# Attention queries and keys in f16 halves, three-product scores, and a new split of the copies of the turned probabilities

## The reference

```python
q = (x @ Wq).reshape(N, S, HEADS, HEAD_DIM).transpose(0, 2, 1, 3)
k = (x @ Wk).reshape(N, S, HEADS, HEAD_DIM).transpose(0, 2, 1, 3)
...
logits = jnp.einsum('nhid,nhjd->nhij', q, k) * scale
causal = 1000000000.0 * (jnp.tril(jnp.ones((S, S), dtype=logits.dtype)) - 1.0)
logits = logits + causal[None, None, :, :]
attn = jax.nn.softmax(logits, axis=-1)
out = jnp.einsum('nhij,nhjd->nhid', attn, v)
```

## Time and profile before

| | |
|---|---|
| median of the runs shown | 890.14 us |
| profiled execution | 890.64 us |
| its span in the profile | 889.4 us |
| TensorE busy in the span | 859.9 us (97%) |
| VectorE busy | 606.1 us (68%) |
| ScalarE busy | 557.2 us (63%) |
| GpSimd busy | 377.8 us (42%) |

### The profile page before, as it was taken

How to read it: one execution, slowest core, us unless ns; L and a number is a source line. 1 busy time by engine, 2 the same in 40 slices (tenths; PEclk the granted TensorE clock), 3 DMA queues, 4 the chain that set the end, 5 groups by cost and what they waited for, 6 DMA issues and landing times. The chain is left out here.

```text
span 889.4 us, 23089 instructions
## 1 busy us (share of the span) xinstructions
PE 859.9 (97%) x8094; PEld 680.0 (76%) x8094; DVE 606.1 (68%) x1669; ACT 557.2 (63%) x1251; POOL 377.8 (42%) x492
## 2 busy tenths in 40 slices
PE   5999999999999999999999999999999999999996
PEld 3888788888888888767676666676788888887864
DVE  3667588776667675756666667869677767766655
ACT  4988776777676776655756565564455555555555
POOL 1634354343433475324444332544534444444433
PEclk9999999999999999999999999999999999999999
DMA  9733424342424331410000000399423323333226
GB/s 317 207 126 113 142 97 152 119 160 96 143 94 138 103 119 49 62 42 2 1 1 1 2 1 1 105 393 356 158 52 50 49 44 50 49 50 50 43 27 195
DMA packets 61579, 88.04 MB, mean 99 GB/s; under 512 B 17279, under 2 KB 46527, under 8 KB 61343
## 3 DMA queue, kind: packets, MB, share of 16 engines
q1 hardware_dynamic: 53439, 75.52, 25.8%
q0 software_dynamic: 7488, 10.27, 7.3%
q10 hardware_dynamic: 544, 0.79, 0.3%
HBM read 56.00 MB, written 30.56 MB: 97 GB/s over the span
## 5 line engine op out<-in xcount | busy, mean ns | idle before, releaser
L648 POOL TENSOR_SCALAR prob<-prob,rden 128x128 f32<-128x128 f32 (+1 forms) x256 | 122.9, 498 | 183.1 <-DVE rden L949 183.0
L2219 PE MATMUL ps<-slots,e 128*128 128x128 f16 x1872 | 190.0, 219 | 2.2 <-DVE xs L2386 2.1
L2219 PEld LDWEIGHTS ps<-slots,e 128*128 x1872 | 152.6, 97 | 35.3 <-issue 4.4
L843 ACT ACTIVATE prob<-prob,nmx 128x128 f32<-128x128 f32 (+1 forms) x256 | 113.2, 444 | 29.8 <-DVE nmx L943 29.8
L2227 PE MATMUL ps<-e,xT 128*128 x312 | 117.3, 378 | 0.0
L2316 ACT ACTIVATE slots<-slots 128x512 f32<-128x512 f32 x78 | 49.1, 630 | 106.8 <-DVE slots L2370 106.8
L943 DVE CUSTOM_DVE_ANT_0 prob<-ps,mask 128x128 f32<-128x128 f32 (+1 forms) x256 | 73.7, 353 | 41.5 <-PE ps L730 41.5
L31 PE MATMUL ps<-xT,wqkv 128*128 128x256 f16 x768 | 97.2, 278 | 2.0 <-ACT slots L850 1.4
L31 PEld LDWEIGHTS ps<-xT,wqkv 128*128 128x128 f16 x768 | 73.4, 99 | 18.3 <-issue 6.9
L1731 POOL DMA_INDIRECT xg<-rows_x,dst x39 | 40.9, 1049 | 106.3 <-DVE mask L2359 103.0
L2228 PE MATMUL ps<-e,xT 128*128 x312 | 85.0, 273 | 0.0
(11 more groups left out here) (267 smaller groups left out, 1855.3 us busy)
## 6 DMA issues: line engine op xcount, KB each, us to landing
halves<-parted SPq DMA_DIRECT2D x36, 512.0 KB, 2.9
piece<-in_L_ffn_ew SPq DMA_DIRECT2D x32, 512.0 KB, 4.5
e<-halves SPq DMA_DIRECT2D x16, 1024.0 KB, 15.2
piece<-in_L_ffn_sh_w SPq DMA_DIRECT2D x4, 512.0 KB, 8.8
sw<-halves SPq DMA_DIRECT2D x4, 512.0 KB, 6.8
rows_x<-xs SPq DMA_DIRECT2D x4, 512.0 KB, 7.4
xs<-back_y SPq DMA_DIRECT2D x8, 256.0 KB, 4.4
out<-xs SPq DMA_DIRECT2D x8, 256.0 KB, 2.1
```

Of the source, the lines that this page charges most:

```text
L648: PO.tensor_scalar(prob[u][:, h, r], prob[u][:, h, r], rden[u][:, h, t:t + 1], 1.0, ALU.mult, ALU.mult).then_inc(normed, 1)
L843: SC.activation(at, at, ACT.Exp, bias=nmx[u][:, h, t:t + 1], scale=-1.0, accum_out=den[u][:, h, t:t + 1]).then_inc(exped, 1)
L2219: yield PE.matmul(ps[:, 2 * u + q, (k % 4) * P:(k % 4) * P + P], w[ch][h], xgT[u][j][:, ch, :], start=n == 0, stop=n == 3 * DC - 1)
```

## The change

Queries and keys leave the PSUM bank as two f16 parts. ScalarE writes the high part, and a new VectorE operation subtracts it from the bank and writes the low part, after which the semaphore `qk_lo` says that the item is there and the bank is free. The scores are the three f16 products of `HILO` in place of one float32 product. ScalarE copies three of four heads' turned probabilities and VectorE one. On ScalarE the even item's copy stands ahead of the second pair's exponentials in all stages, and the squares of the context are spread over stages 4 to 9. On VectorE the odd item's low part stands behind `add_projection`, and the scaling of the context moves from stages 9 to 12 to stages 11 to 13.

```diff
@@ -312,6 +312,9 @@
 
         FOLDED = [(wb, wbh, r, slice(0, G3), WS) for r in range(DC)] + [
             (pnT, pnh, r, slice(k * half, (k + 1) * half), 1.0) for k in range(2) for r in range(DC)]
+        ROOTED_AT = 10
+        SQUARED_AT = {4: (0,), 5: (1,), 6: (2,), 7: (3,), 8: (4, 5), 9: (6, 7)}
+        SCALED_AT = {11: (0, 1, 2), 12: (3, 4, 5), 13: (6, 7)}
         FOLDED_AT = {26: (0,), 27: (1,), 28: (2,), 29: (3, 4), 30: (5,)}
 
         def folded_high(q):
@@ -461,7 +464,8 @@
             wo = [sb(c, f"wo{i}", [P, PAIRS, D], F16) for i in range(2)]
             bo = sb(c, "bo", [P, D])
             zrow = sb(c, "zrow", [P, D + 2])
-            qk = [part(slots_flat, 4 * 3 * DC * GT + 8 * S * i, 2 * S).rearrange("p (k t) -> p k t", k=2) for i in range(2)]
+            qk = [[part(slots_flat, 4 * 3 * DC * GT + 8 * S * u + 4 * S * i, 2 * S, F16).rearrange("p (k t) -> p k t", k=2)
+                   for i in range(2)] for u in range(2)]
             v_sb = [sb(c, f"v{i}", [P, S // P, 2, P]) for i in range(2)]
             prob = [sb(c, f"prob{i}", [P, 4, 384]) for i in range(2)]
             pT = sb(c, "pT", [P, 4, 384])
@@ -667,7 +671,7 @@
                         normalise(j + 1, 1)
                     if batch_ending(j) is not None and j < LAST:
                         root(batch_ending(j))
-                    if j == 8:
+                    if j == ROOTED_AT:
                         context_root()
                     for q in FOLDED_AT.get(j, ()):
                         folded_high(q)
@@ -704,7 +708,7 @@
                 def project_qk(n):
                     b, cols = n // PAIRS, slice(n % PAIRS * P, n % PAIRS * P + P)
                     if n >= 1:
-                        PE.wait_ge(qk_out, n)
+                        PE.wait_ge(qk_lo, n)
                     if n % PAIRS == 0:
                         PE.wait_ge(x_hi, b + 1)
                         PE.wait_ge(x_lo, b + 1)
@@ -723,12 +727,13 @@
                     if m >= 2:
                         PE.wait_ge(pT_out, 2 * (m - 1))
                     for p in range(2):
-                        PE.wait_ge(qk_out, 2 * m + p + 1)
+                        PE.wait_ge(qk_lo, 2 * m + p + 1)
                         for t in range(2):
-                            for h in range(2):
-                                r = slice(HD * h, HD * h + HD)
-                                mm = PE.matmul(ps[:, 2 + 2 * p + h, query_tile(t)], qk[p][r, 0, t * P:t * P + P],
-                                               qk[p][r, 1, 0:(t + 1) * P], start=True, stop=True)
+                            for n, (i, j) in enumerate(HILO):
+                                for h in range(2):
+                                    r = slice(HD * h, HD * h + HD)
+                                    mm = PE.matmul(ps[:, 2 + 2 * p + h, query_tile(t)], qk[p][i][r, 0, t * P:t * P + P],
+                                                   qk[p][j][r, 1, 0:(t + 1) * P], start=n == 0, stop=n == len(HILO) - 1)
                         mm.then_inc(s_mm, 1)
 
                 def weigh_values(m):
...
@@ -847,14 +852,14 @@
                     SC.wait_ge(qk_mm, n + 1)
                     if n >= 2:
                         SC.wait_ge(s_mm, n - 1)
-                    SC.mul(qk[n % 2][:, :, :], ps[:, 0, :].rearrange("p (k t) -> p k t", k=2), 1 / WS).then_inc(qk_out, 1)
+                    SC.mul(qk[n % 2][0][:, :, :], ps[:, 0, :].rearrange("p (k t) -> p k t", k=2), 1 / WS).then_inc(qk_hi, 1)
 
                 def probs_turned(m):
 
                     SC.wait_ge(p_turned, 2 * m + 2)
                     if m >= 1:
                         SC.wait_ge(o_mm, m)
-                    SC.copy(pT[:, 2:4, :], ps[:, 4:6, 0:384]).then_inc(pT_out, 1)
+                    SC.copy(pT[:, 1:4, :], ps[:, 3:6, 0:384]).then_inc(pT_out, 1)
 
                 def values_out(m):
                     SC.wait_ge(v_mm, m + 1)
@@ -885,24 +890,23 @@
                         vw_high(1)
                     if 0 <= j - 1 < STAGES:
                         heads_high(j - 1)
-                    if j <= 0:
+                    if j + 2 < STAGES:
                         queries_keys(2 * (j + 2))
                     if 0 <= j + 1 < STAGES:
                         exponentials(j + 1, 1)
-                    if 0 < j < STAGES - 2:
-                        queries_keys(2 * (j + 2))
                     if 0 <= j < STAGES:
                         probs_turned(j)
                     for q in high_at.get(j, ()):
                         piece_high(q)
-                    if SHARES <= j < 2 * SHARES:
-                        context_squares(2 * (j - SHARES))
-                        context_squares(2 * (j - SHARES) + 1)
+                    for b in SQUARED_AT.get(j, ()):
+                        context_squares(b)
                     if share_at(j) is not None and share_at(j) >= KEYS:
                         prep_scalar(share_at(j), 6)
+                    if j < 0:
+                        queries_keys(2 * (j + 2) + 1)
                     for i in HIGH_AT.get(j, ()):
                         weight_high(i)
-                    if j + 2 < STAGES:
+                    if 0 <= j < STAGES - 2:
                         queries_keys(2 * (j + 2) + 1)
                     if j == LAST - 1:
                         high_part(0)
@@ -943,6 +947,11 @@
                             VE.tensor_tensor_reduce(prob[u][:, h, r], ps[:, 2 + h, r], mask[:, r], -SCALE, HIGHEST,
                                                     ALU.add, ALU.min, nmx[u][:, h, t:t + 1]).then_inc(masked, 1)
 
+                def queries_keys(n):
+                    VE.wait_ge(qk_hi, n + 1)
+                    VE.scalar_tensor_tensor(qk[n % 2][1][:, :, :], ps[:, 0, :].rearrange("p (k t) -> p k t", k=2), 1 / WS,
+                                            qk[n % 2][0][:, :, :], ALU.mult, ALU.subtract).then_inc(qk_lo, 1)
+
                 def reciprocals(m, p):
                     u, h = m % 2, slice(2 * p, 2 * p + 2)
                     VE.wait_ge(exped, 8 * m + 4 * (p + 1))
@@ -953,7 +962,7 @@
                     VE.wait_ge(p_turned, 2 * m + 1)
                     if m >= 1:
                         VE.wait_ge(o_mm, m)
-                    VE.tensor_copy(pT[:, 0:2, :], ps[:, 2:4, 0:384]).then_inc(pT_out, 1)
+                    VE.tensor_copy(pT[:, 0, :], ps[:, 2, 0:384]).then_inc(pT_out, 1)
 
                 def heads_low(m):
                     slot = 2 * (m % DOUBLES)
@@ -1006,6 +1015,8 @@
                         reciprocals(j + 1, 0)
                     if 0 <= j - 1 < STAGES:
                         heads_low(j - 1)
+                    if j + 2 < STAGES:
+                        queries_keys(2 * (j + 2))
                     if 0 <= j < STAGES:
                         probs_turned(j)
                     if 0 <= j + 1 < STAGES:
@@ -1017,23 +1028,26 @@
                         prep_vector(share)
                     for q in FOLDED_AT.get(j - 1, ()):
                         folded_low(q)
+                    if j < 0:
+                        queries_keys(2 * (j + 2) + 1)
                     for i in LOW_AT.get(j, ()):
                         weight_low(i)
                     for n in low_shares.get((j, 1), ()):
                         piece_low(n)
+                    if batch_ending(j) is not None and j < LAST:
+                        add_projection(batch_ending(j))
+                    if 0 <= j < STAGES - 2:
+                        queries_keys(2 * (j + 2) + 1)
                     for n in low_shares.get((j, 2), ()):
                         piece_low(n)
                     if j == 5:
                         context_biases()
-                    if j == 8:
+                    if j == ROOTED_AT:
                         context_mean()
-                    if 9 <= j < 9 + NB // 2:
-                        context_scale(2 * (j - 9))
-                        context_scale(2 * (j - 9) + 1)
+                    for b in SCALED_AT.get(j, ()):
+                        context_scale(b)
                     if batch_turned(j) is not None:
                         inputs_low(batch_turned(j))
-                    if batch_ending(j) is not None and j < LAST:
-                        add_projection(batch_ending(j))
                 low_part(0)
                 add_projection(NB - 1)
                 vw_low(2)
```

4 lines of the change are left out of this document (2 added, 2 removed).

## The result

The changed kernel takes 899.65 us (median of 4 runs, 898.52 to 901.63), the kernel before 888.59 us beside it (4 runs, 886.86 to 892.16). The ratio is 1.0126 with a 95% interval of 1.0104 to 1.0148: slower by 1.3%, 11.1 us. I had forecast 896 us, 6 us more than before: the right side, in the range, and 5 us short of the 11.1 measured.

What follows compares the result with a forecast made beforehand. TensorE was taken to bound the kernel: scores -9.6, waits of before -4.9, new waits +15.3 and start +3.5 gave +4.3 us; a late load (0.5) and the clock (1.3) made it +6, so 896 us, range 882 to 904.

Steps and rivals of the forecast that it cites:

- the odd item's chain: ScalarE and VectorE, two-piece stages: second pair can start at 10.76 us, TensorE wants it at 9.82 to 10.68.
- The list of waits: TensorE's new waits by stage: 7.2 us in stages 2 to 9, 5.7 in 10 to 17, 2.4 from 18; together 15.3.
- The scores' term: Scores on TensorE: three f16 products take 0.99 us instead of 1.30, 0.30 less a step, 9.6 us in 32 steps.
- Late loads and the clock: Left out of the chains: a late load worth 0.5 us and a fallen clock worth 1.3, raising the sum to +6.
- The scaling of the context: VectorE, stages 12 to 14: scalings of 0.395 us each ahead of the masks do not fit, beside whh of 1.3 us.
- The start: Ahead of the loop: stage 1 starts 2.8 us late and waits another 0.75; 3.5 us more, bounds 0 and 4.
- waits of before: Losses of the kernel before in stages 1 to 9, taken to go: 4.9 us less.
- The rival with smaller waits: Waits in the 20 waiting stages are 0.3 us smaller each, the sum cancels: 890 us; chance of same 0.27.
- the rival with the low part hidden: VectorE's low part is hidden, only plain two-piece stages wait, some 4 us with the start: 881 us; chance 0.19.
- the rival in which the f16 halves do not overlap: Scores on TensorE cost 0.7 us more per stage, 22 us: about 913 us; f16 without its gain has chance 0.06.

Runs made afterwards that it cites:

- Experiments 2: The changed kernel with a stage's second piece on ScalarE behind the odd item's copy; 887.69 us, ratio 0.9986 to the kernel before.
- experiment 4: The changed kernel with squares, root and scaling of the context in the stages of the kernel before; 902.72 us, ratio 1.0155.
- experiment 3: The changed kernel with the odd item's low part ahead of `add_projection` on VectorE; 903.58 us, ratio 1.0153.
- experiment 8: The kernel before, without f16 parts, with only the second piece of a stage moved behind the odd item's copy; 885.98 us, ratio 0.9959.
- experiment 10: The changed kernel with second piece behind the odd copy, and root, scaling, weights' parts and quarter shares in other places; 884.66 us, ratio 0.9953.
- 6: The changed kernel with ScalarE and VectorE each copying two heads of turned probabilities; 898.00 us, ratio 1.0102.
- 5: The changed kernel with ScalarE's even copy back behind the second exponentials in the stages from 1 on; 905.25 us, ratio 1.0182.
- 7: The changed kernel with context work, heads' copies and even copy as before, low part kept; 908.12 us, ratio 1.0212.
- 1: The kernel before with f16 high parts alone and three high-by-high score products, no low part, not to reference precision; 879.33 us, ratio 0.9891.

## Why the prediction was right in kind and too small

**The mechanism held.** I had the odd item's chain (three heads' copy, two pieces, high part, low part) as what TensorE would wait for. It is the line that the waits name. In stage 15 the odd copy starts 9.43 us after the scores (predicted 9.38) and the low part ends at 10.73 (10.76). I had stages 18 to 25 nearly free of waits, and only stage 25 has one, of 0.34. The list of waits, stage by stage:

| stages | predicted | measured |
|---|---|---|
| 2 to 9 | 0.99, 0.59, 1.44, 0.36, 1.31, 0.52, 1.41, 0.53 | 0.91, 1.07, 3.46, 0, 0.67, 0.38, 1.51, 0.30 |
| 10 to 17 | 1.01, 0, 1.09, 1.89, 0.60, 0.05, 0.51, 0.55 | 0.78, 0, 2.29, 1.73, 0, 0, 0.49, 0.33 |
| 18 to 25 | about 0 | 0, and 0.34 in stage 25 |
| from 26 on | 2.4 with the above | 0, 0, 1.49, 1.10 |

Among the stages behind two pieces the chain was right to a tenth in stages 2, 8 and 16. It was 0.2 to 0.6 us too long in 6, 10 and 14, and too short where a load came late (4 and 12). I had named stages 12 and 13 as the worst; the worst is stage 4. Experiments 2 and 8 show that the second piece ahead of the copy is the cause of most of it: without it 6.0 of the 17.3 us are left.

**The scores' term was too small, which was in the change's favour.** "-0.30 us a step" measured -0.41: 13.1 us in 32 steps and not 9.6. My term was the difference of the issue alone (1.30 to 0.99). The distance from the scores' start to the values' start fell from 1.51 to 1.09, and a stage without a wait from 10.04 to 9.63. The Trainium skill ("TensorE: Matmul & The Clock Gate", LDWEIGHTS) gives columns / 1.2 ns for a weight load, 107 ns for 128 columns. Twelve such loads one behind another in each row half would be 1.28 us, an estimate by that figure, and no gain. A single load is near it, 0.092 to 0.096 us for the first ten of a step, but all 24 are done within 0.89 us, so they do not stand one behind another; the measurement decides.

**A wait costs more than its length.** I priced a wait as the time that TensorE stands. Where the two pairs run through, the scores are one group of 1.16 us; where the second waits, they are two groups of 0.67 with the wait between, so that 0.67 + 0.67 - 1.16 = 0.18 us comes on top. Stage 16, which waits 0.49, shows it: 10.29 - 0.49 - 0.18 = 9.62, and stage 15 without a wait took 9.63. For sixteen waits that is 2.9 us, which my sum had not.

**Late loads and the clock were too small.** I had 0.5 us for late loads. In stage 3 the second piece's load came 1.33 us after ScalarE was free and in stage 11 it was 1.90 us; behind them stages 4 and 12 waited 2.0 and 1.2 us longer than predicted. Stage 12 in the changed kernel:

```profile
152.43 0.67 PE L735 MATMUL ps<-slots 64*128 64x128 f16 x12
153.06 1.06 ACT L586 ACTIVATE parted<-piece 128x1024 f16<-128x1024 f32 x1 [1.90 <-DMA piece<-in_L_ffn_ew]
154.03 0.58 ACT L855 ACTIVATE slots<-ps 128x512 f16<-128x512 f32 x1
...
154.64 0.69 DVE L952 SCALAR_TENSOR_TENSOR slots<-ps,slots 128x512 f16<-128x512 f32 x1 [2.96 <-ACT slots L855]
...
155.39 0.67 PE L735 MATMUL ps<-slots 64*128 64x128 f16 x12 [2.29 <-DVE slots L952]
```

Nothing of VectorE's is in the way here (it had been idle for 2.96 us); it is the load, then the piece, then the two halves of the copy. For the fallen clock I had 1.3 us. TensorE was busy for 12.22 us in stage 4 and for 9.63 in stage 15 (one turns inputs, the other has a share, 0.43 each); 0.18 of the difference is the split, so the clock cost about 2.4.

**The scaling of the context was wrong as a cause.** I had put it among the causes of the waits of stages 12 and 13. Three scalings take 0.87 us together there, not 3 x 0.395, and taking them back shortened the waits of stages 12 and 13 by only 1.3 us, while the kernel got no faster (experiment 4). Stage 13 waits as long as I said (1.73, predicted 1.89), behind whh and `add_projection`: the low part ends at 166.89. With the low part ahead of `add_projection` (experiment 3) stage 13 has no wait.

**The start was about right.** Stage 1 starts 2.0 us late (predicted 2.8) and waits 0.49 (0.75). From 16 to 34 us TensorE waits 1.5 us in two waits for the weights' low parts that I named (line 935), but more, 2.9 us in three waits, for the low part of queries and keys, where it had waited 1.2 us in two for ScalarE's copy.

**The sum again, with what was measured.** Stages 1 to 29: scores 29 x -0.41 = -11.9; waits of before removed -4.9 (as predicted); new waits 17.3 + 0.7; their splits +2.9; the clock +2.4. That is +6.5, where the windows have +7.05. The start adds 2.0, so 8.5 of the 9.2 us in the span are accounted for. That the waits of before were worth 4.9 has support in experiment 8, where stages 1 to 29 are 4.7 us shorter. The medians differ by 11.1, since the profiled execution of before, at 890.64 us, was one of its slower ones.

So the mechanism was right, and what failed is the step for what the chains leave out ("The chains hold no late load and no fallen clock"), which I took at 0.5 and 1.3 us. Behind the late loads stages 4 and 12 waited 3.2 us longer than predicted, the clock cost 2.4, and the splits, which my sum had at nothing, 2.9: together 6.7 us more than I had. The scores brought 2.3 us more than I had (11.9 in 29 steps against 9.6 in 32), and the start and the other waits 2 us less of a loss. That the sum came out only 3 us too small in the span is in part luck, since these errors had opposite signs. The medians' 11.1 us hold 2 us more for the reason above. The rival with smaller waits had the single chains looser than they are; the rival with the low part hidden is ruled out as written, and with other places the low part is mostly hidden in stages 1 to 29 (experiment 10) but its 881 is not reached in the whole (884.66); the rival in which the f16 halves do not overlap is ruled out by the 1.16 us.

What stays open: of the low part's cost the 5.8 us of longer busy time are splits and clock together, and I have not parted them. Why experiment 3's clock fell once more was not tried, nor a kernel with a PSUM bank for each of the two items, in which a low part would not stand between two projections; whether a bank can be had for it I have not looked.

## What to carry to other kernels

When a bank's copy becomes two operations on two engines in series, the cost is not their duration but the slack of the last item behind which they stand: list what is queued ahead of each of the two, in every kind of stage, and move what nobody waits for (here the second piece, 12 us) before you judge the change. Anything that waits for a load should stand behind, not ahead of, an operation that the bounding engine waits for. Price a wait with what it adds around itself, the broken overlap and the clock, and measure the pure gain in a kernel that leaves the new cost out: here it told that at most some 10 us were to be had. Read a small difference between two kernels by the stretch that was changed, and not by the whole time alone: the 4.8 us of experiment 10 over experiment 8 are gone in the total.

## What the runs showed of the hardware

- Matmuls on rows 0 to 63 and 64 to 127 overlap in f16 as they do in float32: 24 products, 4608 columns in all counting both halves, 1.16 us from first start to last end, while twelve f16 products on all 128 rows, 3072 columns, take 1.49 us.
- With TensorE's stand of 3.46 us in stage 4 the granted clock fell from 2.4 to 1.2 GHz for 6.8 us; with stands of 2.29 and 1.73 us in stages 12 and 13 it did not (clock 1.00 in the window of stages 11 to 13). Before the change it fell with one of 1.75 us, for 3.4 us. The experiments' traces add stands of 3.60, 3.67 and 3.67 us (3, 4, 6), with 6.8 us at half each, and stands of 3.10, 3.05, 2.42, 2.32 and 2.29 us (5, 7, 1, 3, 7), with 3.4 us each. So the length of the stand alone does not tell: of two of 2.29 us one came with a fall and one did not.
- ScalarE's copy from PSUM took 1.10 us for 1152 columns and 0.80 for 768, in proportion less than the columns. So the third head costs 0.30. VectorE's low part of 512 columns took 0.69 us in the mean of 64.
